# A conditioned feed-forward kernel: another order of VectorE's and TensorE's work in the first two groups

## The reference

```python
q_emb = relu(cond @ W3 + b3)                       # one row per batch
x1 = (64 * x + sum_over_tokens(x)) * q_emb         # per batch
y  = relu(x1 @ W2 + b2)
gates = softmax(y @ W_router + b_router)           # six experts, the best two are kept
h  = y @ A_r                                       # six experts of rank 16
routed = (h * kept gates) @ B_r
out = x + (y @ W_base + b_base) + (y @ A_s) @ B_s + routed
```

## Time and profile before

| | us |
|---|---|
| median of 3 runs | 237.95 (237.94 to 238.31) |
| the profiled execution's own time | 237.04 |
| its span, first to last instruction | 235.2 |
| TensorE busy | 229.3 (97%) |
| VectorE busy | 166.7 (71%) |
| ScalarE busy | 86.2 (37%) |
| GpSimd busy | 49.0 (21%) |

### The profile page before, as it was taken

One profiled execution on the slowest core, in us unless ns is written; L12 is line 12 of the kernel. 1 busy time (PEld: TensorE's weight loads), 2 busy tenths in 40 slices (PEclk: granted clock), 3 DMA queues, 4 the chain that ended last, 5 costly groups with the idle time before them and its releaser, 6 DMA issues.

```text
span 235.2 us, 3088 instructions
## 1 busy us (share of the span) xinstructions
PE 229.3 (97%) x1006; PEld 186.9 (79%) x1006; DVE 166.7 (71%) x309; ACT 86.2 (37%) x171; POOL 49.0 (21%) x57
## 2 busy tenths in 40 slices
PE   7999899999999999999999999999999999999994
PEld 3977687788888888888888888888888888888883
DVE  0794997798979967497838969299665976064344
ACT  3369451534136330444206340263305351252330
POOL 6288422012132211023012120022111130000000
PEclk9999999999999999999999999999999999999999
DMA  6999903527053632717044541709020370104004
GB/s 214 340 219 227 253 4 71 142 99 261 11 137 65 222 137 37 175 70 289 8 117 89 187 172 22 185 4 329 28 33 0 126 231 13 22 0 178 3 0 178
DMA packets 32505, 28.80 MB, mean 122 GB/s; under 512 B 5817, under 2 KB 22909, under 8 KB 32494
## 3 DMA queue, kind: packets, MB, share of 16 engines
q1 hardware_dynamic: 30682, 28.50, 42.4%
q10 hardware_dynamic: 1812, 0.17, 0.6%
HBM read 18.89 MB, written 8.39 MB: 116 GB/s over the span
## 4 chain that ended last, share of the span: by engine, by line
PE 87%; SPq 6%; DVE 2%; DMA 2%; issue 0%; DVEq 0%
PE m_ps L747 78%; PE hT L747 9%; SPq L210 3%; DMA x_quart<-in_x_dram 2%; DVE out_nat L625 1%; SPq L226 1%; SPq L233 1%; SPq L229 1%; DVE xT L471 0%; SPq L231 0%; DVE vsum L476 0%; DVE x_sum L483 0%; SPq L237 0%; DVE y_lo L497 0%; SPq L236 0%
## 5 line engine op out<-in xcount | busy, mean ns | idle before, releaser
L308 POOL TENSOR_TENSOR x_full<-x_sum,qT 128x512 f32<-128x512 f32 x28 | 32.4, 1156 | 136.7 <-DVE x_sum L483 136.7
L353 ACT ACTIVATE y_hi<-m_ps,condT 128x512 fp32r<-128x512 f32 x32 | 21.9, 686 | 80.4 <-PE m_ps L747 80.2
L747 PE MATMUL m_ps<-Wb_lo,y_hi 128*128 128x512 f32 x128 | 49.8, 389 | 0.0
L747 PE MATMUL m_ps<-Wb_hi,y_hi 128*128 128x512 f32 x128 | 49.8, 389 | 0.0
L747 PE MATMUL m_ps<-Wb_hi,y_lo 128*128 128x512 f32 x128 | 49.8, 389 | 0.0
L747 PE MATMUL m_ps<-x_hi,W_hi 128*128 128x512 f32 x112 | 43.8, 391 | 0.0
L747 PE MATMUL m_ps<-x_hi,W_lo 128*128 128x512 f32 x112 | 43.6, 389 | 0.0
L747 PE MATMUL m_ps<-x_lo,W_hi 128*128 128x512 f32 x112 | 43.6, 389 | 0.0
L497 DVE TENSOR_TENSOR y_lo<-m_ps,y_hi 128x512 fp32r<-128x512 f32 x32 | 21.7, 677 | 30.3 <-ACT m_ps L355 30.3
L471 DVE STREAM_TRANSPOSE xT<-x_quart 128x512 f32<-128x512 f32 x28 | 30.3, 1084 | 3.0 <-DMA x_quart<-in_x_dram 3.0
L747 PEld LDWEIGHTS m_ps<-Wb_hi,y_lo 128*128 128x128 f32 x128 | 24.0, 188 | 5.0
(11 more groups left out here) (99 smaller groups left out, 255.1 us busy)
## 6 DMA issues: line engine op xcount, KB each, us to landing
out_dram<-out_nat SPq DMA_DIRECT2D x32, 256.0 KB, 2.3
x_quart<-in_x_dram SPq DMA_DIRECT2D x28, 256.0 KB, 4.5
x_nat<-in_x_dram SPq DMA_DIRECT2D x7, 1024.0 KB, 6.2
gatesT<-wT SPq DMA_DIRECT2D x28, 48.0 KB
x_nat<-in_x_dram SPq DMA_DIRECT2D x4, 256.0 KB, 3.4
W_f<-in_L_cond_W_dram SPq DMA_DIRECT2D x4, 256.0 KB, 6.0
Wb_f<-in_L_ffn_W_base_dram SPq DMA_DIRECT2D x1, 1024.0 KB, 8.7
W_sb<-in_L_cond_W_dram SPq DMA_DIRECT2D x2, 256.0 KB, 4.2
```

Source lines behind the costliest of these rows:

```text
L308: nc.gpsimd.tensor_tensor(per_batch(x1_full[:, c, :]), per_batch(x1_sum[:, c, :]), qT[:, c, bass.ds(BG * g, BG)].unsqueeze(2).to_broadcast ...
L353: nc.scalar.activation(y_hi[:, m, :], m1_ps[m][:, :], ACT.Relu, bias=b2_sb[:, m:m + 1]).then_inc(y_hi_ready, 1)
L747: mm = nc.tensor.matmul(psum, lhsT, rhs, start=start and i == 0, stop=stop and i == len(terms) - 1)
```

## The change

In the head: one more warm matmul while x loads and one more behind the third q column; ScalarE makes q_relu(1) ahead of W2_split(0), q_relu(2) ahead of x_hi of chunk 0 and q_relu(3) ahead of x_hi of chunk 1. In `m1_first`, the products of chunk 0 are taken for tiles 0 to 2 first (hi x hi, then W2_lo x hi), those of tile 3 behind them.

In the first group VectorE takes each y_rest ahead of a step for the next x, and the turn and total of chunk 2 go behind the gates. ScalarE rounds chunk 0 of the next x ahead of h_head, and its pick copies go to the second group, behind the relus.

In the second group TensorE takes, in the new `m1_second`, all products with x_hi of tiles 0 to 2 chunk by chunk, waiting for x_hi alone, and then those with x_lo tile by tile. VectorE begins with weigh, hw_rest and the addition of the first finished output tile (tile 2), and each y_rest comes behind that, ahead of a step for the next x; y_rest(3) goes ahead of the total of chunk 1 and of rest(0). ScalarE makes hw_hi ahead of the relus. The arithmetic is the same; the steady groups are as before.

```diff
--- before.py
+++ after.py
@@ -46,7 +46,7 @@
     SH = 16
     RO = 32
 
-    WARM_LOAD, WARM_W3, WARM_HALF, WARM_Q = 7, 1, 2, 1
+    WARM_LOAD, WARM_W3, WARM_HALF, WARM_Q = 8, 1, 2, 2
     assert ONE < SH and SH + R <= RO and RO + E * R == P and TT == KC and NG % 2 == 0 and NG >= 4
 
     x_groups = x.rearrange("b n d -> (b n) d").rearrange("(g t p) d -> g p t d", t=TT, p=P)
@@ -378,12 +378,12 @@
                 nc.scalar.activation(x1_hi[0][:, c, :], head_ps[c][:, :], ACT.Copy).then_inc(x1_hi_ready, 1)
 
             q_relu(0)
+            q_relu(1)
             W2_split(0)
-            q_relu(1)
+            q_relu(2)
             x1_split_head(0)
-            q_relu(2)
+            q_relu(3)
             x1_split_head(1)
-            q_relu(3)
             W2_split(1)
             W2_split(2)
             x1_split_head(2)
@@ -423,15 +423,19 @@
                     if not last:
                         x1_split(g + 1, 1 - par, c)
 
+                if second:
+                    hw_split(slice(0, TG), g)
                 for m in range(KC):
                     relu(g, m, first)
-                    if m == 0 and not first:
+                    if m == 0 and not first and not second:
                         hw_split(slice(0, TG), g)
                     if not first and m >= (2 if second else 1):
                         split(m - (2 if second else 1))
                 if first:
                     act.wait_ge(Wu_loaded, 48)
                     nc.scalar.activation(Wu_hi[:, :], Wu_f[:, :], ACT.Copy).then_inc(Wu_hi_ready, 1)
+                    split(0)
+                if second:
                     pick_round()
 
                 act.wait_ge(h_done, g + 1)
@@ -443,7 +447,6 @@
                 if last:
                     nc.scalar.activation(h_sb[:, :], hT[:, :], ACT.Identity, bias=h_bias[:, 0:1]).then_inc(h_ready, 1)
                 if first:
-                    split(0)
                     split(1)
                 if second:
                     split(2)
@@ -648,31 +651,28 @@
                     hw_rest(slice(0, TG), g)
 
                 if first:
+                    y_rest(g, 0)
                     turn(0)
+                    y_rest(g, 1)
                     total(0)
+                    y_rest(g, 2)
+                    turn(1)
+                    y_rest(g, 3)
+                    total(1)
+                elif second:
+                    weigh_before()
+                    hw_rest_before()
+                    add_x(g - 1, 1 - par, UP_TILES[:1], 0)
                     y_rest(g, 0)
-                    turn(1)
+                    turn(0)
                     y_rest(g, 1)
-                    sum_x(g + 1, 1)
-                    y_rest(g, 2)
-                    add_sum(g + 1, 1)
-                    y_rest(g, 3)
-                    turn(2)
-                    total(2)
-                elif second:
-                    y_rest(g, 0)
-                    weigh_before()
-                    turn(0)
                     total(0)
-                    hw_rest_before()
-                    y_rest(g, 1)
-                    turn(1)
-                    add_x(g - 1, 1 - par, UP_TILES[:1], 0)
                     y_rest(g, 2)
                     add_x(g - 1, 1 - par, UP_TILES[1:], 1)
+                    turn(1)
+                    y_rest(g, 3)
                     total(1)
                     rest(0)
-                    y_rest(g, 3)
                     rest(1)
                     turn(2)
                     total(2)
@@ -698,11 +698,13 @@
                 rank_experts(g)
                 gates(g, last)
                 if first:
-                    rest(0)
+                    turn(2)
+                    total(2)
                 if first or second:
                     turn(3)
                     total(3)
                 if first:
+                    rest(0)
                     rest(1)
                 rest(2)
                 rest(3)
@@ -775,12 +777,24 @@
                                             start=k == 0 and W is W2_hi and x1 is x1_hi,
                                             stop=k == KC - 1 and x1 is x1_lo)
 
-                for k in range(KC // 2):
+                pe.wait_ge(x1_hi_ready, 1)
+                pe.wait_ge(W2_hi_ready, 1)
+                for m in range(KC - 1):
+                    pe.wait_ge(qT_ready, m + 1)
+                    chunk(m, 0, W2_hi, x1_hi)
+                pe.wait_ge(W2_lo_ready, 1)
+                for m in range(KC - 1):
+                    chunk(m, 0, W2_lo, x1_hi)
+                pe.wait_ge(qT_ready, KC)
+                chunk(KC - 1, 0, W2_hi, x1_hi)
+                chunk(KC - 1, 0, W2_lo, x1_hi)
+                pe.wait_ge(x1_lo_ready, 1)
+                for m in range(KC):
+                    chunk(m, 0, W2_hi, x1_lo)
+                for k in range(1, KC // 2):
                     pe.wait_ge(x1_hi_ready, k + 1)
                     pe.wait_ge(W2_hi_ready, k + 1)
                     for m in range(KC):
-                        if k == 0:
-                            pe.wait_ge(qT_ready, m + 1)
                         chunk(m, k, W2_hi, x1_hi)
                     pe.wait_ge(W2_lo_ready, k + 1)
                     for m in range(KC):
@@ -800,6 +814,23 @@
                             if k == KC - 1:
                                 last.then_inc(m1_done, 1)
 
+            def m1_second():
+
+                x_hi, x_lo = x1_hi[1], x1_lo[1]
+                for k in range(KC):
+                    pe.wait_ge(x1_hi_ready, KC + k + 1)
+                    for m in range(KC - 1):
+                        cols = slice(m * P, (m + 1) * P)
+                        product(m1_ps[m][:, :], [(W2_hi[:, k, cols], x_hi[:, k, :]),
+                                                 (W2_lo[:, k, cols], x_hi[:, k, :])], k == 0, False)
+                for m in range(KC - 1):
+                    cols = slice(m * P, (m + 1) * P)
+                    for k in range(KC):
+                        if m == 0:
+                            pe.wait_ge(x1_lo_ready, KC + k + 1)
+                        mm = product(m1_ps[m][:, :], [(W2_hi[:, k, cols], x_lo[:, k, :])], False, k == KC - 1)
+                    mm.then_inc(m1_done, 1)
+
             def h(g, k, first):
 
                 if k == 0 and first:
@@ -858,7 +889,9 @@
                 if first:
                     m1_first()
                 else:
-                    for m in range(KC - 1):
+                    if second:
+                        m1_second()
+                    for m in () if second else range(KC - 1):
                         m1(g, par, m)
                     up(UP_TILES, g)
                     m1(g, par, KC - 1)
```

## The result

The changed kernel has a median of 242.06 us (240.22 to 242.93, 4 runs) where the kernel before has 237.94 (237.47 to 238.31, 4 runs): a ratio of 1.0164, 95% interval 1.0101 to 1.0227. It is slower, as forecast, but by 4.1 us and not by 2.1. The profiled execution is the shortest of the four, 240.22, with a span of 238.3 and a full clock.

The account below looks back on a forecast made before the run. TensorE, busy 97% of the span at a full clock, was taken as the bound. Its terms, -1.72 - 0.58 + 0.47 + 3.90 = +2.07 us on the median of 237.95, gave 240.0 us, range 239.0 to 241.5.

Parts of the forecast that it names:

- The first group's 1.72 us: TensorE's loss in the first group, mostly waiting for y_lo; with y_rest taken first, all 1.72 us go.
- group 1's 0.58: TensorE's loss in group 1, which takes 27.78 instead of 27.20; x_hi products first were to win all 0.58 us.
- the 15 instructions: VectorE's work from the addition of tile 2 to the end of x rest(0): 2 turns and 13 others, 10.1 us.
- The added wait: VectorE stands 2.9 us for tile 2's addition, rest(3) starts at 68.8, and TensorE loses 3.90 us at group 2.
- the 0.87 of the logit: Logit subtraction on VectorE, slowed beside GpSimd's scaling, stays at 0.87 us; if they missed each other, the result would be 239.3.
- The two waits of TensorE at group 2: TensorE idles about 2 and 1.6 us near 65 to 70, for x_lo of chunks 2 and 3.
- VectorE held at its queue: Nothing behind tile 2's addition starts early; the rival that VectorE isn't held gave 237.1, chance 0.07 of a faster kernel.
- The head: Warm matmuls and ScalarE's new order at the start: 0.47 us lost, between 0 and 0.6.
- x_lo of chunk 2 makes a wait: In the head, that x_lo ends at 17.75 and its matmul starts at 17.90 instead of 17.65.
- a fall of the clock: Rival: the clock falls in the two waits at group 2, 1.5 us more, 241.5; chance 0.10.
- the wait ahead of 24.36: First-group wait of TensorE of over 1 us that left the clock full, taken as evidence against a clock fall.
- the warm-up's 3.3 us: Length assumed for the low-clock stretch, from the warm matmuls: 7.7 matmuls x 0.2 = 1.5 us more.

Follow-up runs that it names:

- turn_ahead: The changed kernel with turn(0) and total(0) ahead of the addition of tile 2 in VectorE's second group; 238.06 us, ratio 1.0014 to the kernel before.
- vector_order: The changed kernel with VectorE's second group in an order near the old one, TensorE and ScalarE as changed; 235.95 us, ratio 0.9929 to the kernel before.
- before_again: The kernel before, unedited, profiled once more; one execution of 238.04 us, span 236.0.
- head_alone: The kernel before with the head's edits alone (warm matmuls, ScalarE's order, products of chunk 0); 238.13 us, ratio 1.0013.
- after_again: The changed kernel run and profiled once more, unedited; 241.60 us median, ratio 1.0149 to the kernel before.
- second_alone: The kernel before with the second group's edits alone, head and first group left as before; 243.72 us, ratio 1.0244.
- fill: The changed kernel with 8 and 6 unused warm matmuls ahead of TensorE's waits for chunks 2 and 3 of group 2; 239.97 us, ratio 1.0102 to the kernel before.

## Why the prediction was right, and where it fell short

- **The gains.** The first group's 1.72 us went, as forecast: 13.60 from h to group 1. Of group 1's 0.58, 0.42 is lost again in another place (the group takes 27.62): the product at 55.01 waits for y_lo(3). The prediction followed y_rest(3) on VectorE only as a part of the 15 instructions and never set it against h(3), which wants it at 54.5; it costs nothing here, because group 2 waits for VectorE anyway.
- **The added wait.** Right in place and size. Forecast from group 1's start to the addition of tile 2: 45.67 - 36.62 = 9.05; measured 46.82 - 37.28 = 9.54. The product was drawn as ended at 46.29 and VectorE started 0.53 later, where I had 0.04. From there to rest(3) 23.14 were forecast and 23.06 measured, with every stretch of the earlier trace rows unchanged, the 0.87 of the logit among them. From the start of rest(3) to TensorE's matmul 0.85 were forecast and 0.74 measured. The two waits of TensorE at group 2 were forecast near 2 and 1.6 us and are 1.91 and 1.33 as the profile draws them, 2.07 and 1.49 from start to start less a regular step of 0.227.
- **GpSimd and the logit.** The rule of the Trainium skill that GpSimd contends with VectorE instructions of two SBUF inputs (GPSIMD Engine Reference, "8. Key points") and the trace agree: scaling began at 61.87 in the changed kernel, and the logit at 62.08 took 0.87 again.
- **VectorE held at its queue.** The strict order that the Trainium skill states (TensorE: Matmul & The Clock Gate, "Architectural detail: the array is 16× 32×32, not 1× 128×128") is borne out by the 2.92 us of idle, and by turn_ahead and vector_order, which win it back.
- **The head.** Forecast +0.47; against before_again h is later by 23.68 - 23.41 = 0.27, which is inside the spread of single profiles; head_alone gives 0.35 with an interval from 0 to 0.6. The reading that x_lo of chunk 2 makes a wait was right (a pause at 18.6 in the changed kernel).
- **The sum at a full clock.** Forecast +2.07. The changed kernel's three executions at 1.000 took 240.07, 240.22 and 240.31, against 237.78: +2.3 to +2.5. Term by term against before_again: head +0.27 (forecast +0.47), first group -1.60 (-1.72), group 1 -0.20 (-0.58), group 2 +3.88 (+3.90), together +2.35, and group 3 starts 95.98 - 93.63 = 2.35 later. By these terms most of the difference stands in group 1, but the 0.4 lost in h(3) has no price of its own: VectorE fixes chunk 3 of group 2, 33.34 behind the start of group 1 where the forecast has 69.65 - 36.62 = 33.03. These 0.3 are the late addition, 9.54 - 9.05, less the 0.08 and the 0.1 of the stretches behind it; a smaller head takes 0.2 back, and the rest is smaller still. So the forecast of 240.0 is right for these executions to 0.2 us, in part by luck, since a head and a VectorE path that were each off by some tenths went against each other.
- **The step that failed is the clock's.** The sum held nothing for a fall of the clock. The prediction named it in the right place as a rival, gave it 1 in 10 and 1.5 us, and drew the evidence against it from the wait ahead of 24.36, which is one wait of over a microsecond with full work on both sides. At group 2 two waits stand with three matmuls between. The fall came in 7 of 10 executions and cost 1.4 to 2.7 us (241.59 to 242.93 against the 240.20 of those with a full clock), 2.2 in the profile of after_again. The price was taken from the warm-up's 3.3 us; the slow stretch was 6.83 us long in both profiles that caught one. The wait hides what lies ahead of its end, 2 us of that stretch in after_again. Both the chance and the size were too small, and together they are the whole distance between 240.0 and 242.06 but for 0.2.

## What to carry to other kernels

An instruction that waits for a far engine is paid by everything behind it in the queue: before moving one forward, read when its input can be there and what could run in between; here two steps in front of the wait were worth 2.1 us at a full clock, and the right order 5.7 us of the median (241.60 to 235.95). If a change makes TensorE wait twice in a short stretch, the clock belongs in the sum (here about 2 us on top of waits of 3.6 in all), and matmuls without a use into a free bank are a cheap cover while the wait is there. A forecast from one profile should be held against the spread of the other runs: its head was 0.8 us earlier than in the second profile. Here that cost little, because the forecast added differences to the median and not to that profile's time.

## What the runs showed of the hardware that I had not expected

- In after_again the granted clock was still full at the end of the first wait (1.91 us) and fell at 68.70, in the first of the three matmuls behind it; in second_alone it fell at 70.88, in the second wait. It then stayed at 1.2 GHz through 4.8 us (after_again) and 6.0 us (second_alone) of work without a pause. With matmuls in the gaps it stayed at 2.4 GHz in five of five executions. The single wait of 1.2 us in the first group left it full.
- The first addition on VectorE started 0.53 us behind the drawn end of its product wherever VectorE stood idle for it (changed kernel; 0.54 in after_again, fill and second_alone), and 0.1 behind it in turn_ahead, where VectorE had been at work. No run here shows why. The prediction's 0.04 comes from hand-overs to ScalarE.
